# Residual and gate move from the Mamba stage to the attention stage; attention turns its keys at the end of the body before

## The reference, cut to what matters

```
# layer 0 (Mamba)
shift, scale, gate = split(silu(c) @ ada_w.T + ada_b, 3)
xn    = layernorm(x) * (1 + scale) + shift
x_ssm = mamba(xn)                 # in_proj, causal conv of 4 taps, SiLU, x_proj, dt, scan over time with 16 states, gate z, out_proj
x1    = x + gate[:, None, :] * x_ssm
# layer 1 (linear attention with FiLM)
xn = layernorm(x1)
q, k, v = xn @ Wq + bq, xn @ Wk + bk, xn @ Wv + bv
k = where(mask, -inf, k);  v = where(mask, 0, v)
q = softmax(q over the 32 channels of a head);  k = softmax(k over time)
attn = einsum('bhse,bhsd->bhed', k, v);  y = einsum('bhtd,bhed->bhte', q, attn)
h = layernorm(y) * (1 + scale2) + shift2
out = x1 + silu(h) @ film_out_W + film_out_b
```

## Time and profile before

| | |
|---|---|
| median of 3 runs | 5054.49 us (5052.17 to 5054.73) |
| the profiled execution | 5058.92 us, its span 5057.1 us |
| Mamba, about 75 to 3803 us | POOL about 99% busy, DVE 94%, PE 88%, ACT 73% |
| attention, about 3803 to 5057 us | PE 94% busy, DVE 61%, ACT 34%, POOL 25% |
| TensorE's granted clock | 0.969 of full speed over the span |

### The profile page before, as it was taken

The page is one execution under the profiler, slowest core; times in us unless marked ns, Lnnn a source line. Parts: engine busy times, 40 slices in busy tenths (PEclk is TensorE's granted clock), DMA queues, the critical chain, the costliest instruction groups (busy, mean ns, idle before and its releaser), DMA issues. The chain is left out here.

```text
span 5057.1 us, 75222 instructions
## 1 busy us (share of the span) xinstructions
PE 4449.8 (88%) x21856; PEld 3181.9 (63%) x21856; DVE 4197.5 (83%) x5075; ACT 3086.4 (61%) x7493; POOL 3938.8 (78%) x1861
## 2 busy tenths in 40 slices
PE   7798988888888888888888988888877999999997
PEld 4666666666666666666666666666654655655654
DVE  2999999999999999999999999999984665665654
ACT  2777777777777767777777777777652333333332
POOL 0999999999999999999999999999981222222222
PEclk8999999999999999999999999999978999999999
DMA  5111111112211111111211111111102111111111
GB/s 189 44 51 54 55 53 51 52 60 68 68 51 52 57 51 53 52 59 60 71 57 52 55 53 53 52 52 62 60 25 77 50 40 54 40 40 54 40 40 44
DMA packets 117994, 284.78 MB, mean 56 GB/s; under 512 B 15905, under 2 KB 21281, under 8 KB 117090
## 3 DMA queue, kind: packets, MB, share of 16 engines
q1 hardware_dynamic: 117602, 280.13, 16.8%
HBM read 245.35 MB, written 34.73 MB: 55 GB/s over the span
## 5 line engine op out<-in xcount | busy, mean ns | idle before, releaser
L646 POOL TENSOR_TENSOR dbu<-du,bc 128x1024 f32<-128x1024 f32 x1024 | 2411.6, 2389 | 114.7 <-DVE du L584 114.7
L407 ACT ACTIVATE dA<-dt,c_A 128x256 f32<-128x256 f32 x4096 | 1754.4, 468 | 609.2 <-DVE hC L547 483.2
L613 DVE TENSOR_TENSOR_SCAN hS<-dA,dbu 128x512 f32<-128x512 f32 x1024 | 1209.8, 1208 | 168.8 <-PE Y L288 114.8
L657 POOL TENSOR_TENSOR hS<-hS,bc 128x1024 f32<-128x1024 f32 x512 | 1223.8, 2390 | 22.8 <-DVE hS L613 22.8
L613 DVE TENSOR_TENSOR_SCAN dA<-dA,dbu 128x512 f32<-128x512 f32 x1024 | 1205.0, 1211 | 25.4 <-ACT dA L407 18.4
L288 PEld LDWEIGHTS Y<-c_ident,hC 128*128 128x128 f32 x4096 | 484.5, 144 | 284.8 <-DVE hC L547 188.0
L288 PE MATMUL Y<-c_ident,hC 128*128 128x128 f32 x4096 | 555.9, 280 | 121.5 <-DVE hC L547 117.9
L547 DVE TENSOR_TENSOR hC<-dA,bc 128x1024 f32<-128x1024 f32 x512 | 626.6, 1224 | 22.4 <-DVE dA L613 5.7
L329 PE MATMUL side<-c_in_w,xnF 128*128 128x512 f32 x1024 | 537.3, 651 | 119.7 <-DVE u L576 80.0
L346 PE MATMUL side<-xnF,c_in_w 128*128 128x256 f32 x2048 | 491.2, 384 | 81.5 <-DVE zs L568 49.0
L288 PE MATMUL Y<-c_ident,hS 128*128 128x128 f32 x4096 | 542.3, 276 | 15.9 <-POOL hS L657 15.9
(11 more groups left out here) (124 smaller groups left out, 5841.2 us busy)
## 6 DMA issues: line engine op xcount, KB each, us to landing
bc<-b_scratch SPq DMA_DIRECT2D x256, 512.0 KB, 4.1
x_in<-in_x SPq DMA_DIRECT2D x32, 512.0 KB, 5.2
gb<-gate_scratch SPq DMA_DIRECT2D x64, 256.0 KB, 4.1
xres<-in_x SPq DMA_DIRECT2D x64, 256.0 KB, 3.6
x_scratch<-xres SPq DMA_DIRECT2D x64, 256.0 KB, 2.0
p_x_in<-x_scratch SPq DMA_DIRECT2D x32, 512.0 KB, 4.0
p_xr<-x_scratch SPq DMA_DIRECT2D x32, 512.0 KB, 4.1
out<-p_xr SPq DMA_DIRECT2D x32, 512.0 KB, 3.1
```

The costliest lines, as they stand in the source:

```text
L407: last = act.activation(dA[:, q % A_RING, e, :], dt[j % 2][:, e, :], ACT.Exp, scale=C["A"][:, 2 * j + e, n:n + 1])
L613: dve.tensor_tensor_scan(out.rearrange("p e t -> p (e t)"), dA[:, q % A_RING, :, :].rearrange("p e t -> p (e t)"), dbu[(q // 2) % B_RING][ ...
L646: gps.tensor_tensor(dbu[p % B_RING][:, :, :, :], du[j % 2][:, :, :].unsqueeze(1).broadcast_to([P, 2, 2, GT]), bc[:, 0, n:n + 2, :].unsquee ...
L657: gps.tensor_tensor(h, h, bc[:, 1, n:n + 2, :].unsqueeze(2).broadcast_to([P, 2, 2, GT]), ALU.mult).then_inc(hcP_done, 1)
```

## The change

In Mamba the output projection is no longer multiplied by the gate nor added to x. ACT copies the PSUM bank to one of two tiles `oS`, two units after PE's last piece, and SP stores it to a DRAM scratch `o`. DVE's L571, POOL's L673 and the loads of gate and x go.

In attention SP loads, for each group, `o`, the gate's two rows and x; POOL multiplies and adds them at the head of its body (S part), into `x_in`. SP stores x1 to DRAM and `xr` is loaded from there as before. These loads are issued one group ahead, behind the store of x1.

The turn of the keys moves from the head of body g to the end of the body before: first sequence behind the second film product, second sequence behind the last query product. ACT's kT copies stand between the two exponentials of the queries. On PE the two halves of the key product now have the turn of q between them. One body more is written out at the end instead of looped.

```diff
-D_AFTER = {"Z": 4, "CV": 4, "DT": 4, "O": 2}
-G_AFTER = {"O": 4}
+A_AFTER = {"Z": 2, "CV": 2, "DT": 2, "XN": 2, "XI": 2, "XP": 2, "O": 2}
+D_AFTER = {"Z": 4, "CV": 4, "DT": 4}
...
+    oS = [sb(f"oS{i}", [P, D]) for i in range(GB)]
...
         def keep(sp, gq, b):
 
-            n = gq * GB + b
-            sp_wait(sp, x1_done, n + 1)
-            sp.dma_start(io["x1"][bass.ds(n, 1), :, :].rearrange("b t d -> (b t) d"), xres[:, :]).then_inc(x1_stored, 16)
+            sp_wait(sp, og_done, gq * GB + b + 1)
+            sp.dma_start(io["o"][bass.ds(gq * GB + b, 1), :, :].rearrange("b t d -> (b t) d"), oS[b][:, :]).then_inc(o_stored[b], 16)
...
+            elif kind == "O":
+                wait(act, o_stored[j], 16 * own)
+                act.activation(oS[j][:, :], src[:, :], ACT.Copy).then_inc(og_done, 1)
...
-            elif kind == "O":
-                wait(dve, gate_loaded, own * 32 + 16 * (j + 1))
-                dve.tensor_tensor(gb[:, :], src[:, :], gb[:, :], ALU.mult).then_inc(og_done, 1)
...
-                        gps.tensor_tensor(xres[:, :], xres[:, :], gb[:, :], ALU.add).then_inc(x1_done, 1)
...
-        with eng.Fori(0, NG - 4) as i:
+        with eng.Fori(0, NG - 5) as i:
...
+        def load_x(sg):
+            sp.dma_start(o_in[:, :, :], io["o"][bass.ds(sg * GB, GB), :, :].rearrange("b t d -> t b d")).then_inc(s["x_loaded"], 16)
+            sp.dma_start(g_in[:, :, :], io["gate"][bass.ds(sg * GB, GB), :].partition_broadcast(P)).then_inc(s["x_loaded"], 16)
+            sp.dma_start(x0[:, :, :], io["x"][bass.ds(sg * GB, GB), :, :].rearrange("b t d -> t b d")).then_inc(s["x_loaded"], 16)
+
         def body(g, S, A, B, Cc):
             sg, a, c = g + 2, g + 1, g - 1
-            if S:
-                sp_wait(sp, s["ln1_done"], sg * GB)
-                sp.dma_start(x_in[:, :, :], io["x1"][bass.ds(sg * GB, GB), :, :].rearrange("b t d -> t b d")).then_inc(s["x_loaded"], 16)
             if isinstance(g, int) and g == -2:
+                load_x(0)
                 load_weights()
             if A:
                 sp_wait(sp, s["mask_done"], a)
...
+            if S:
+                sp_wait(sp, s["x1_done"], sg + 1)
+                sp.dma_start(io["x1"][bass.ds(sg * GB, GB), :, :].rearrange("b t d -> t b d"), x_in[:, :, :]).then_inc(s["x1_stored"], 16)
+                if not (isinstance(g, int) and sg + 1 >= NG):
+                    load_x(sg + 1)
             if Cc:
+                sp_wait(sp, s["x1_stored"], c * 16 + 16)
                 sp_wait(sp, s["out_stored"], c * 16)
                 sp.dma_start(xr[:, :, :], io["x1"][bass.ds(c * GB, GB), :, :].rearrange("b t d -> t b d")).then_inc(s["xr_loaded"], 16)
...
# PE, attention: the turn of the keys goes from the head of the body ...
-            if B:
-                for b in range(GB):
-                    wait(pe, s["es_done"], g * 2 + 2)
-                    wait(pe, s["f_done"], g * 2 + (b - 3))
-                    for k in range(KD):
-                        last = pe.transpose(banks[0][b][:, k * P:(k + 1) * P], k_e[:, k, b * P:(b + 1) * P], ident)
-                    last.then_inc(f["ET"], 1)
...
+            if A:
+                keys(0)
             if B:
                 for b in range(GB):
                     wait(pe, s["qe_done"], g * 2 + (b + 1))
                     wait(pe, s["v_done"], g * 2 + (b + 1))
                     turn(banks[2][b], q[:, b, :]).then_inc(f["QT"], 1)
+            if A:
+                keys(1)
...
+            def turn_keys(b):
+                wait(pe, s["es_done"], a * 2 + 2)
+                wait(pe, s["f_done"], c * 2 + (b + 1))
+                for k in range(KD):
+                    last = pe.transpose(banks[0][b][:, k * P:(k + 1) * P], k_e[:, k, b * P:(b + 1) * P], ident)
+                last.then_inc(f["ET"], 1)
...
             if A:
+                turn_keys(0)
                 queries(1)
+                turn_keys(1)
...
# ACT, attention
-            if B:
-                for b in range(GB):
-                    wait(act, f["ET"], g * 2 + (b + 1))
-                    act.activation(kT[:, b, :], banks[0][b][:, :], ACT.Copy).then_inc(s["kT_done"], 1)
...
+                exp_queries(0)
+                keep_keys(0)
+                keep_keys(1)
+                exp_queries(1)
...
# POOL, attention
-            a, c = g + 1, g - 1
+            sg, a, c = g + 2, g + 1, g - 1
+            if S:
+                wait(gps, s["x_loaded"], sg * 48 + 48)
+                gps.tensor_tensor(o_in[:, :, :], o_in[:, :, :], g_in[:, :, :], ALU.mult).then_inc(s["gated"], 1)
+                wait(gps, s["gated"], sg + 1)
+                wait(gps, s["ln1_done"], sg * GB)
+                wait(gps, s["x1_stored"], sg * 16)
+                gps.tensor_tensor(x_in[:, :, :], o_in[:, :, :], x0[:, :, :], ALU.add).then_inc(s["x1_done"], 1)
```

More of the change, by code:

```diff
@@ L143, in mamba @@
     Y = ctx.enter_context(nc.psum_tensor("Y", [P, GB, 2 * P], F32))
[L146 to L147 removed]
+    x_loaded, b_stored = (sem(n) for n in ("x_loaded", "b_stored"))
+    o_stored = [sem(f"o_stored{b}") for b in range(GB)]
     b_loaded = [sem(f"b_loaded{k}") for k in range(4)]
@@ L278, in _ @@
         over_groups(sp, body)
-        sp.wait_ge(x1_stored, 16 * NG * GB)
+        for b in range(GB):
+            sp.wait_ge(o_stored[b], 16 * NG)
     @block.tensor
@@ L503, in body @@
                         copy_dt(j, bank[bk], go + d)
-                    if kind in ("XN", "XI", "XP") and q == end + A_AFTER[kind] - off:
+                    if kind in ("XN", "XI", "XP", "O") and q == end + A_AFTER[kind] - off:
                         simple(kind, j, bank[bk], go + d, (of + d) % 2)
@@ L667, in body @@
                             readout(g - t // PAIRS, j, m)
-                for kind, j, d, slots in SIDE:
-                    if kind == "O" and (slots[-1] + G_AFTER[kind]) // 2 + 2 == p and inside(at, d):
-                        n = (g + d) * GB + j
-                        wait(gps, og_done, n + 1)
-                        wait(gps, xres_loaded, n * 16 + 16)
-                        gps.tensor_tensor(xres[:, :], xres[:, :], gb[:, :], ALU.add).then_inc(x1_done, 1)
         over_groups(gps, body)
@@ L695, in attention @@
     heads = sb("heads", [P, P])
+    o_in, g_in, x0 = (sb(n, [P, GB, D]) for n in ("o_in", "g_in", "x0"))
     x_in = sb("x1_in", [P, GB, D])
@@ L740, in over_groups @@
             peeled(g)
-        with eng.Fori(0, NG - 4) as i:
+        with eng.Fori(0, NG - 5) as i:
             body(i + 2, True, True, True, True)
-        for g in range(NG - 2, NG + 1):
+        for g in range(NG - 3, NG + 1):
             peeled(g)
@@ L831, in body, with keys @@
                     pe.wait_ge(s["w_in"], 16 * 11)
-                for j in range(2):
-                    wait(pe, s["xn_done"], a * 2 + 2)
-                    for e in range(2):
-                        for k in range(KD):
-                            m = (2 * j + e) * P
-                            last = pe.matmul(banks[1][j][:, e * GT:(e + 1) * GT], wk[:, k, m:m + P], xnF[:, k, :],
-                                             start=(k == 0), stop=(k == KD - 1))
-                    last.then_inc(f["K"], 1)
+            def keys(j):
+                wait(pe, s["xn_done"], a * 2 + 2)
+                for e in range(2):
+                    for k in range(KD):
+                        m = (2 * j + e) * P
+                        last = pe.matmul(banks[1][j][:, e * GT:(e + 1) * GT], wk[:, k, m:m + P], xnF[:, k, :],
+                                         start=(k == 0), stop=(k == KD - 1))
+                last.then_inc(f["K"], 1)
+            if A:
+                keys(0)
             if B:
@@ L937, in body, with exp_queries, keep_keys @@
             if A:
-                for b in range(GB):
+                def exp_queries(b):
                     wait(act, s["qsub_done"], a * 2 + (b + 1))
                     act.activation(q[:, b, :], q[:, b, :], ACT.Exp).then_inc(s["qe_done"], 1)
+                def keep_keys(b):
+                    wait(act, f["ET"], a * 2 + (b + 1))
+                    wait(act, f["AT"], g * 2 + (b + 1))
+                    act.activation(kT[:, b, :], banks[0][b][:, :], ACT.Copy).then_inc(s["kT_done"], 1)
+                exp_queries(0)
+                keep_keys(0)
+                keep_keys(1)
+                exp_queries(1)
         over_groups(act, body)
@@ L992, in body @@
             if S:
-                wait(dve, s["x_loaded"], sg * 16 + 16)
+                wait(dve, s["x1_done"], sg + 1)
                 for b in range(GB):
```

18 lines of the change are left out of this document (5 added, 13 removed).

## The result

The changed kernel takes 4977.15 us (median of 4, 4975.1 to 4978.5), the kernel before 5054.61 beside it: ratio 0.985, 95% interval 0.983 to 0.986. The forecast was 4968, range 4930 to 5009. The profiled spans differ by 5057.1 - 4975.0 = 82.1 us, for which the forecast had 86.

| | before | after | gain | forecast |
|---|---|---|---|---|
| Mamba: to the issue of attention's first load | 3805.07 | 3763.08 | 42.0 | 57.3 |
| from there to the first key product | 21.2 | 32.3 | -11.1 | -12 |
| from the first key product to the end | 1230.9 | 1179.6 | 51.3 | 41 |

The account below looks back on a forecast made before the run. Mamba was taken as bound by POOL, with DVE nearly a second bound, and attention by PE. Terms 56 + 1.3 + 41 - 12 give 86 us, so 5054.5 - 86 = 4968 us, range 4932 to 5009.

Parts of the forecast that it names:

- Mamba's gain per group: Mamba loop: each group gets 1.8 us shorter, between 1.4 and 2.46; 56 us in 31 groups.
- the lower end: Mamba group: if DVE with its fixed waits is the bound, gain 1.4 us (43 us in 31 groups).
- Mamba's end: Last Mamba group: its second residual add, on the path alone, leaves; gain 1.3 us.
- the upper end: Mamba group: if POOL stays the bound, gain 2.46 us (76 us in 31 groups).
- ACT's copy at nothing: Mamba: ACT's copy out of PSUM, about 0.5 us twice per group, costs nothing because PE has ended earlier.
- Attention's order: Attention body: PE's 2.10 us wait before L819 goes, 1.2 us before key product comes; period 36.15, gain 41 us overall.
- The residual in attention: Head of attention body: POOL's product and add, 5.0 us, and xr coming 12 us late stay hidden.
- The margin of hF: Attention body: hF is ready 1.4 us before the film product needs it; beyond that each us costs one per body.
- The mask: Attention body: DVE's mask waits only for the end of POOL's product, 0.8 us; hp and ht come 0.3 us late.
- the rival of 5037: Attention body: mask held through both POOL instructions, period 0.9 us longer than today; time 5037 us; chance 5%.
- The start of attention: Start of attention: POOL waits for all weights, then residual and norm follow; 12 us lost once, ends 8 and 15.
- The slow rival: Head of attention body: five transfers run one after another, 21 us, body 47.5 us; time 5310 us; chance 4%.

## Why the forecast held, and where it didn't

- **Mamba's gain per group** is the step that failed, and by the forecast's own sign: "I take 1.8, nearer to the lower end". The first and the last layer norm of Mamba, some 30 groups apart, stand 29.6 us closer, 1.0 per group, below even the lower end of 1.4 (26 to 32 us with the scatter between executions). A group takes 113.4 us, where the forecast called itself wrong above 113. The lower end kept DVE's waits for PE fixed ("These don't shrink when POOL gets faster"). They grew: per group DVE's work fell by 1.17 us (3012.90/28.0 to 3004.54/28.2), and its idle rose by 0.24. POOL's rows close the same sum: its work fell by 2.3 us per group, its waits for DVE rose from 0.7 to 2.1 (18.7/28.0 and 58.6/28.2), which leaves 0.9. Nearly all of these waits stand behind a turn of the loop. Shown, by the kernels with half the turns, is that the turn of the loop is on the path and that the change uncovered it; only with four groups in a turn a group takes the forecast's 112.4 us (3200 us and 1367 instructions of POOL at 48). That ACT's waits add to it is only read from the list. The sign was in the earlier trace rows: a longest wait of 7.2 us where the mean is 3.6.
- **Mamba's end** gave back part of it: 42.0 - 29.6 = 12.4 us, for which the forecast had 57.3 - 30 x 1.8 = 3.3. From 3400 to 3600 us POOL is busy 200.00 of 200 in both kernels, so there the upper end holds; and from POOL's last readout to the first load it is 24.4 us instead of 29.0. What makes up the rest of the 12.4 is open; 3 us are within the scatter of the mark.
- **ACT's copy at nothing**: the result right, its cover wrong. It waits up to 0.9 us for PE; what hides it is ACT's own slack behind DVE.
- **Attention's order**: right in mechanism and nearly in size. The key product starts 5.28 us behind the last query product (4501.26 - 4495.98; forecast 5.4), the value product 13.16 (13.2), the body is 35.99 (36.15). Of the 10 us more than forecast, 0.16 us in each of 31 bodies are 5. Another 5 are three bodies of 39.0 to 39.1 us that the kernel before has, 1.6 longer than the others, where PE came back from its wait of 2.0 to 2.1 us at a lower clock, 0.57 or 0.58 over the next 4 us in all three. The forecast priced the wait and not what can follow it.
- **The residual in attention**: hidden, as forecast, shown by 1230.5 beside 1230.9 us with the old order. POOL waits 9.9 us for xr, forecast 8, and starts on it 17.5 us behind the last query product, forecast 16.7. The margin of hF was therefore 0.6 us (first half ready at 4517.2, wanted at 4517.8) and not 1.4. It held, narrowly. The term that was short is the transfers': 4528.6 + 1 + 6.7 is 4536.3 and not the forecast's 4536.8, so 7.7 to 8.2 us from the issue of the store to the landing of xr. Measured are 9.6: SP takes 2.8 us to issue the four ahead (4503.88 to 4506.64), and xr then lands in 6.8. Nor is the price beyond the margin one us per us: a wait of 2.1 us cost 85.8/28 = 3.1 us per body with two more loads.
- **The mask**: it started during POOL's product (4498.67 to 4501.03), took 0.56 us (its median in the kernel before is 0.29) and ended 0.15 after it; POOL's add began 0.24 us after the product, and 0.07 where the two don't meet (3784.09 + 2.34 to 3786.50, at the start). One instruction is waited for and not two. The trace agrees here with the Trainium skill, "SBUF — State Buffer", section "SBUF: two separate sides"; the rival of 5037 falls.
- **The start of attention**: 11.1 us for 12. Its main part, POOL's wait for all weights, is shown by the kernel that lacks it (8.4 us).
- **The slow rival**: transfers overlap. The issue to landing of xr rose from 4.1 to 6.8 us, where five in a row would be 21. How late xr lands goes with what is issued ahead of it: 3.6 us with nothing, 6.8 behind four, and 2.8 more behind six. That agrees with the ring order in "DMA: Bandwidth & Descriptors" of the Trainium skill, section "Queues, rings and completion order", which has descriptors taken up in ring order but doesn't promise that they finish in it; it could be shared bandwidth alone.

## What to carry to other kernels

When work leaves the busiest engine, ask what its work was hiding: a stop that comes once per turn of a loop doesn't show in averages, and it takes the gain of exactly those engines that have become faster. Look at the longest wait of each row beside the mean one, and compare the place behind the turn with the same place in the middle. And price a wait of TensorE of 2 us with the clock behind it, not by its length alone.

## What was not expected of the hardware

PE stops for 2.5 to 3.8 us at each turn of Mamba's loop in the changed kernel and those made from it, mostly 2.7 to 3.1: every 227 us with two groups in a turn, every 450 with four, and with fourteen once, 3.17 us at 1793.87. In the kernel before the stops are 2.6 to 4.2 us, with four groups in a turn 2.8 to 4.6. What PE does in that time no view shows.

A wait of PE of 2.1 us is sometimes followed by the lower clock and sometimes not. Here the kernel before, in one of its three long bodies (columns as in the last table):

```profile
4290.00:4295.00 5.00, 5.00 (x21) 2.80 (x20) 1.65 (x3) 0.34 (x1) 0.00 (x0) 1.00 0.49 150
4295.00:4300.00 5.00, 2.89 (x17) 2.66 (x16) 2.34 (x7) 3.42 (x7) 2.33 (x3) 0.78 0.61 191
4300.00:4305.00 5.00, 5.00 (x30) 4.67 (x30) 3.94 (x10) 0.79 (x3) 1.22 (x1) 0.88 0.00 0
```

PE is idle for 2.11 us in the second row, and the granted clock is 0.78 and then 0.88. In the kernel before 27 of its 31 waits of 2.0 to 2.1 us in attention have a granted clock of 1.00 over the 4 us behind them, the other four 0.57 to 0.65. With two more loads, where the waits are 1.8 to 2.3 us, it is 0.57 to 0.68 behind 12 of 28. Behind the waits of 0.95 us with the new order alone no body is long. What decides is open.
